# The last two stages of an eight-part transformer kernel: experts' weights merged beside layer norms, the experts' bias by a one-row matmul, sums read from PSUM, the output stored by groups

## The reference

```
x = x + L3_xattn(LN(x), ctx_2048)           # ends in LN(.) * ln_scale + ln_bias, eps 1e-6
x = x + L3_ffn(LN(x))                       # below

y1 = _ln(x + _mha(x, in_proj_w, ...), ln1_g, ln1_b)
gates = softmax(y1 @ wg)                    # 2048 x 8
idx = argmax(gates)                         # one expert for each token, 256 tokens at most for each
h = einsum('ecd,edf->ecf', disp, w1) + b1[:, None, :]
y = einsum('ecf,efd->ecd', h, w2) + b2[:, None, :]
out = where(keep, gate_val * y[slot], 0)
y2 = _ln(y1 + out, ln2_g, ln2_b)
```

## Time and profile before

| | |
|---|---|
| median of 3 runs | 4094.75 us (4091.4 to 4101.48) |
| the profiled execution | 4094.75 us, of which the span (first to last instruction) 4093.0 us |
| busy share | TensorE 89%, VectorE 66%, ScalarE 55%, GpSimd 33% |
| granted TensorE clock, mean | 0.935 of full speed |
| cross attention's end to the span's end | 3832.4 to 4093.0 us, 260.6 us or 6.4% of the span |

### The profile page before, as it was taken

The page is one execution under the profiler, slowest core; times in us unless marked ns, Lnnn a source line. Parts: engine busy times, 40 slices in busy tenths (PEclk is TensorE's granted clock), DMA queues, the critical chain, the costliest instruction groups (busy, mean ns, idle before and its releaser), DMA issues. The chain is left out here.

```text
span 4093.0 us, 72451 instructions
## 1 busy us (share of the span) xinstructions
PE 3629.6 (89%) x28012; PEld 2243.5 (55%) x28017; DVE 2716.3 (66%) x4497; ACT 2253.7 (55%) x3885; POOL 1367.2 (33%) x1655
## 2 busy tenths in 40 slices
PE   3699999889699986997889999999999999999554
PEld 2233333478444434675457776777677776776441
DVE  5799999644477736554347666666666666766648
ACT  2599999633277752222146566665666566656220
POOL 3011111230011102210035556655565556556310
PEclk7699999999799986998989999999999999999777
DMA  4422232001256401000010000000000000000010
GB/s 140 130 59 54 49 58 48 21 12 36 65 78 92 67 2 31 2 2 10 12 53 17 1 1 17 1 17 1 17 1 17 1 17 1 1 1 1 7 42 16
DMA packets 117717, 122.90 MB, mean 30 GB/s; under 512 B 19008, under 2 KB 95648, under 8 KB 116992
## 3 DMA queue, kind: packets, MB, share of 16 engines
q1 hardware_dynamic: 104184, 111.20, 12.0%
q10 hardware_dynamic: 13200, 7.16, 0.6%
HBM read 102.51 MB, written 15.68 MB: 29 GB/s over the span
## 5 line engine op out<-in xcount | busy, mean ns | idle before, releaser
L869 DVE TENSOR_REDUCE att_peak.1<-psS 128x1 f32<-128x512 f32 (+1 forms) x1024 | 579.1, 633 | 21.0 <-PE psS L744 14.7
L2098 DVE TENSOR_TENSOR att_highest.1<-att_highest.1,psS 128x1024 f32<-128x1024 f32 (+1 forms) x320 | 356.7, 1115 | 218.1 <-ACT prob_0.1 L2032 111.8
L839 ACT ACTIVATE att_probT.1<-psT 128x512 f32<-128x512 f32 (+1 forms) x682 | 366.6, 568 | 29.6 <-PE psT L773 9.6
L2190 POOL TENSOR_TENSOR key_sums_0.1<-key_sums_0.1,prob_0.1 128x512 f32<-128x512 f32 x256 | 334.5, 1306 | 28.7 <-POOL key_sums_0.1 L2190 0.4
L2190 POOL TENSOR_TENSOR key_sums_1.1<-key_sums_1.1,prob_1.1 128x512 f32<-128x512 f32 x256 | 332.3, 1298 | 32.8 <-ACT prob_1.1 L2038 5.1
L869 DVE TENSOR_REDUCE att_peak.2<-psS 128x1 f32<-128x512 f32 (+1 forms) x512 | 261.7, 568 | 79.1 <-PE psS L744 76.2
L790 PE MATMUL psM<-att_probT.1,quad_values.1 128*9 128x256 f32 (+1 forms) x3840 | 292.6, 382 | 0.2 <-issue 0.2
L744 PE MATMUL psS<-key_stack.1,query_stack.1 64*128 64x512 bf16 (+1 forms) x1024 | 253.6, 379 | 25.0 <-PEq L379 15.9
L2110 DVE TENSOR_REDUCE att_shift.4<-psO 128x4 f32<-128x512 f32 x64 | 44.3, 692 | 319.0 <-PE psO L1941 319.0
L2185 POOL TENSOR_TENSOR key_sums_0.1<-prob_0.1 128x512 f32<-128x512 f32 x64 | 81.8, 1277 | 517.2 <-ACT prob_0.1 L2038 517.2
L2119 DVE TENSOR_TENSOR prob_1.1<-prob_1.1,psO 128x1024 f32<-128x1024 f32 (+1 forms) x256 | 245.7, 1012 | 5.6 <-PE psO L1948 5.6
(11 more groups left out here) (687 smaller groups left out, 7857.2 us busy)
## 6 DMA issues: line engine op xcount, KB each, us to landing
key_stack.1<-key_parts SPq DMA_DIRECT2D x384, 58.0 KB
key_stack.2<-key_parts SPq DMA_DIRECT2D x96, 200.1 KB
ctx_rows.1<-in_ctx_dram SPq DMA_DIRECT2D x8, 1536.0 KB
key_parts<-split_parts.2 SPq DMA_DIRECT2D x8, 1200.8 KB, 7.4
ctx_keys_0.1<-in_ctx_dram ACTq DMA_DIRECT2D x4, 768.0 KB
ctx_keys_1.1<-in_ctx_dram ACTq DMA_DIRECT2D x4, 768.0 KB
query_stack.1<-query_parts SPq DMA_DIRECT2D x192, 16.0 KB
ctx_values_0.1<-in_ctx_dram SPq DMA_DIRECT2D x4, 768.0 KB
```

The lines of the kernel that those rows point to most:

```text
L839: self.k.nc.scalar.activation(probs[:, blks[0]:blks[-1] + 1, :].rearrange("p b q -> p (b q)"), bank[0:w, 0:len(blks) * S], ACT.Exp).then_i ...
L869: self.k.nc.vector.tensor_reduce(self.peak[:, 2 * h + s, c:c + 1], self.score_bank[m % 3][:, 0:w], AX_X, ALU.max).then_inc(self.peak_done. ...
L2098: self.k.nc.vector.tensor_tensor(own, old, new, ALU.max).then_inc(self.raised.sem, 1)
L2190: nc.gpsimd.tensor_tensor(acc, acc, own[:, h, c * BANK:(c + 1) * BANK], ALU.add).then_inc(self.summed.sem, 1)
```

## The change

1. `cross3` no longer loads `ln_scale` and `ln_shift` and no longer norms at its end. A new block, `two_norms_beside_experts`, takes in that norm, its scale, shift and addition to `X`, and the norm of `X` that opens `batch_attention`. The scale, shift and addition go by groups of four tiles (128x512), each followed by the `bn_stats` of its four tiles. Beside it the experts 0 to 3 are merged. SP issues all of the experts' loads (25 DMAs, 4.2 MB: 8 x 512 KB), with scale and shift as its eighth and ninth; ScalarE's queue issues the eleven loads that SP issued before, ahead of the square root.
2. The attention itself is as it was.
3. `norm_beside_experts` does the norm with `ln1_g`, `ln1_b` by groups of four tiles and the transposes of a group as soon as it is ready, with experts 4 to 7 merged beside it.
4. The block that loads `wgate` and `b2` and the merging block are gone. Merging now alternates buffers: the next expert's w1 is transposed before the product of this one, ScalarE copies both products, GpSimd spreads b1, and b2 goes in by a matmul of one row of ones with the row of b2.
5. `apply_experts`: each half of a tile is a 128-row matmul and a second one of one row (ones, 1 x 128, with the merged bias row, 1 x 512) into the same bank; VectorE's eight scaled sums read PSUM, without a copy to SBUF, and the tile's `bn_stats` for the last norm follows them.
6. `last_norm` has no statistics of its own, goes by groups of four tiles, and stores each group (256 KB) when it is added.

The core of the diff:

```
 def cross3 ...
-                     (scale[:], rows(d["L3_xattn_ln_scale"])), (shift[:], rows(d["L3_xattn_ln_bias"]))]
...
-        layer_norm(k, 1e-6, src=k.XN, transposed=False)
-        scale_and_shift(k, k.XN, scale, shift, add_to=k.X)
...
+def dve_scale_and_shift(k, link, norm, g, scale, shift):
+    for t in range(4 * g, 4 * g + 4):
+        last = norm.dve_apply(t)
+    link(last)
+    x = four_tiles(k.XN, g)
+    link(k.nc.vector.tensor_tensor(x, x, over_four(scale), ALU.mult))
+    return k.nc.vector.tensor_tensor(x, x, over_four(shift), ALU.add)
...
+class MergedExperts:
...
+    def pe_product(self, pe, e):
+        nc, out = self.k.nc, self.k.psT[:, e % 2, :]
+        pe.wait_ge(*self.w1_copied(e + 1))
+        if e >= 2:
+            pe.wait_ge(*self.w12_copied(e - 1))
+        for f in range(FT):
+            nc.tensor.matmul(out[:, 0:D], self.w1T[:, e % 2, f, :], self.w2[:, e, f, :], start=(f == 0), stop=(f == FT - 1))
+        pe.wait_ge(*self.b1_spread(e + 1))
+        for f in range(FT):
+            nc.tensor.matmul(out[:, D:2 * D], self.b1x[:, e % 2, f, :], self.w2[:, e, f, :], start=(f == 0), stop=False)
...
+        nc.tensor.matmul(out[:, D:2 * D], self.ones[:], self.b2[:, e * D:(e + 1) * D], start=False, stop=True).then_inc(self.w12_done.sem, 1)
...
+def two_norms_beside_experts(k, experts, scale, shift, loads):
...
+        @block.sync
+        def _(sp):
+            for e in range(2):
+                experts.load(sp, e)
+            for dst, src in ((scale, "L3_xattn_ln_scale"), (shift, "L3_xattn_ln_bias")):
+                sp.dma_start(dst[:], rows(k.dram[src])).then_inc(affine_loaded.sem, 16)
+            for e in range(2, E):
+                experts.load(sp, e)
...
+            old.dve_variance(dve, link)
+            old.dve_invert(dve, link)
+            dve.wait_ge(*affine_loaded(32))
+            for g in range(NT // 4):
+                link(dve_scale_and_shift(k, link, old, g, scale, shift))
+                x = four_tiles(k.X, g)
+                link(nc.vector.tensor_tensor(x, x, four_tiles(k.XN, g), ALU.add))
+                for t in range(4 * g, 4 * g + 4):
+                    last = new.dve_stats(t)
...
+        @block.scalar
+        def _(act):
+            for dst, src in loads:
+                act.dma_start(dst, src).then_inc(loaded.sem, 16)
+            old.act_deviation(act)
+            experts.act_turned(act, 0)
+            experts.act_run(act, 0, EARLY)
...
+        @block.tensor
+        def _(pe):
+            experts.pe_run(pe, 0, EARLY)
+            for g in range(NT // 4):
+                pe.wait_ge(*xn_done(g + 1))
+                turn_tiles(k, pe, g, xt_done)
...
 def apply_experts ...
-                        pe.wait_ge(*biased(n - 3))
-                    nc.tensor.matmul(k.psS[:, n % 4, :], k.XT[:, t * P:(t + 1) * P], w12[:, i * BANK:(i + 1) * BANK],
-                                     start=True, stop=True).then_inc(product.sem, 1)
+                        pe.wait_ge(*added(EB * (n - 3)))
+                    own = slice(EB * i, EB * i + EB)
+                    out = k.psS[:, n % 4, :].rearrange("p (e d) -> p e d", d=D)
+                    nc.tensor.matmul(out, k.XT[:, t * P:(t + 1) * P], experts.both[:, own, 0, :], start=True, stop=False)
+                    nc.tensor.matmul(out, experts.ones[:], experts.both[0:1, own, 1, :], start=False, stop=True).then_inc(product.sem, 1)
...
-                    nc.vector.tensor_tensor(y[:, t % 2, i * BANK:(i + 1) * BANK], k.psS[:, n % 4, :],
-                                            b12[:, i * BANK:(i + 1) * BANK], ALU.add).then_inc(biased.sem, 1)
...
-                    nc.vector.scalar_tensor_tensor(out=x, in0=y[:, t % 2, e * D:(e + 1) * D], scalar=comb[:, t, e:e + 1], in1=x,
+                    nc.vector.scalar_tensor_tensor(out=x, in0=k.psS[:, n % 4, at:at + D], scalar=comb[:, t, e:e + 1], in1=x,
                                                    op0=ALU.mult, op1=ALU.add).then_inc(added.sem, 1)
+                dve.wait_ge(*added(t * E + E))
+                last = norm.dve_stats(t)
```

More of the change, by code:

```diff
@@ new lines, in encoder3 @@
+def encoder3(k):
+    with ExitStack() as mem:
+        affine = {n: k.sb(n, [P, D], ctx=mem) for n in ("ln1_g", "ln1_b", "ln2_g", "ln2_b")}
+        wgate = k.sb("wgate", [P, E], ctx=mem)
+        experts = MergedExperts(k, mem)
+        batch_attention(k, experts, [(t[:], rows(k.dram["L3_ffn_" + n])) for n, t in affine.items()] + [(wgate[:], k.dram["L3_ffn_wg"])])
+        norm_beside_experts(k, experts, affine["ln1_g"], affine["ln1_b"])
+        gates, comb = k.sb("gates", [P, NT, E], ctx=mem), k.sb("comb", [P, NT, E], ctx=mem)
+        softmax_gates(k, mem, wgate[:], None, gates)
+        place_in_order(k, mem, gates, comb)
+        norm = Norm(k, mem, 1e-5, k.XN)
+        apply_experts(k, mem, comb, experts, norm)
+        last_norm(k, norm, affine["ln2_g"], affine["ln2_b"])
@@ L2255, in scale_and_shift, with last_norm @@
+def last_norm(k, norm, scale, shift):
+    nc, chain, ready, stored = k.nc, k.flag("dve_chain"), k.flag("x_added"), k.flag("stored")
+    GROUPS = NT // 4
     with nc.Block() as block:
@@ L2258, in _ @@
             link = Chain(dve, chain)
[L2260 to L2265, removed]
-            link.end()
[L2269 to L2278, removed]
+            norm.dve_variance(dve, link)
@@ L2280, in _ @@
+            norm.dve_invert(dve, link)
+            for g in range(GROUPS):
+                link(dve_scale_and_shift(k, link, norm, g, scale, shift))
+                x = four_tiles(k.X, g)
+                nc.vector.tensor_tensor(x, x, four_tiles(k.XN, g), ALU.add).then_inc(ready.sem, 1)
+            link.end()
         @block.scalar
         def _(act):
-            for g in range(NT // 4):
-                act.wait_ge(*xt_done(g + 1))
-                nc.scalar.copy(k.XT[:, g * BANK:(g + 1) * BANK], k.psS[:, g, :]).then_inc(xt_copied.sem, 1)
@@ L2304, in batch_attention, with _ @@
-def batch_attention(k, loads):
+            norm.act_deviation(act)
+        @block.sync
+        def _(sp):
+            out = k.out.rearrange("b (t p) d -> p (b t) d", p=P)
+            for g in range(GROUPS):
+                sp.wait_ge(*ready(g + 1))
+                sp.dma_start(four_tiles(out, g), four_tiles(k.X, g)).then_inc(stored.sem, 16)
+            sp.wait_ge(*stored(16 * GROUPS))
+def batch_attention(k, experts, loads):
     nc = k.nc
@@ L3538 @@
 STAGES = (cross0, ffn0_and_cross1, coupled1, depool2, latent2, cross3, encoder3,)
-def store(k):
-    nc, stored = k.nc, k.flag("stored")
-    with nc.Block() as block:
-        @block.sync
-        def _(sp):
-            sp.dma_start(k.out.rearrange("b (t p) d -> p (b t) d", p=P), k.X[:]).then_inc(stored.sem, 16)
-            sp.wait_ge(*stored(16))
 def layers_kernel(nc, dram, out, place):
@@ L3570, in layers_kernel @@
             stage(k)
-        store(k)
 _OUT = ((B, S, D), "float32")
```

286 lines of the change are left out of this document (190 added, 96 removed).

## The result

| | before | with the change |
|---|---|---|
| median | 4094.22 us (6 runs, 4091.4 to 4101.48) | 4111.66 us (6 runs, 4102.62 to 4115.19) |
| ratio, 95% interval | | 1.0037 [1.0027, 1.0048] |
| profiled execution | 4094.75 us, span 4093.0 | 4108.38 us, span 4106.4 |
| mean granted clock | 0.935 | 0.926 |

The change is slower, by 0.37%. The forecast was 4090 us with a range of 4072 to 4110; the measured median lies 1.7 us above it.

The account below looks back on a forecast made before the run. VectorE was taken to bound the apply stage (busy 64.44 of 70.7 us). Terms −0.7 + 2.6 + 1.0 − 1.9 − 4.1 − 38.0 + 40.9 − 4.7 = −4.9 from 4094.75 gave 4089.9, say 4090; range 4072 to 4110.

Parts of the forecast that it names:

- the price of the one-row matmul in the apply stage: Apply stage: one-row records cost the same as full ones, 0.855 us at half clock; stage 111.2 us, +40.9.
- Rival 2: Apply stage: changing stationary operand between 128 rows and one costs 0.58 us per half, 18.6 us; total 4108.5; chance 0.10.
- The clock: Apply stage: pairs of one full and one one-row matmul, begun at clock 0.50, stay at 0.50.
- rival 1: Apply stage: clock rises to full after the first tile, stage 59.9 us, total 4039; chance 0.16.
- The rows in use matter: TensorE: busy time alone neither holds nor brings the high clock, shown by 32-row and 64-row matmuls near 0.50.
- The output norm's wait: Block of the two norms: first apply waits for a later root and for scale and shift, +2.6 (+1.6 to +8).
- The queue stall of the earlier trace: Cross attention's start: SP's fourth issue, 4.51 us, stalls whatever it loads; the start's term was −0.7.
- The merging: Merging block ahead of the apply stage: removed, less a barrier, its work covered by the two norm blocks, −38.0.
- the load block: Block between the last copy and the first gate matmul: 4.44 us less one barrier, −4.1.
- the encoder's norm: Encoder's norm by groups: VectorE +1.0, only the last group's transposes and copy behind it −2.9, together −1.9.
- the end: From the last sum to the span's end: 18.5 us instead of 23.25, −4.7 (−6 to −3).
- Rival 3: Norm blocks: merging delays transposes and SP's queue stalls before scale and shift; 4099.5 us, inside the forecast's range, no own chance.

Follow-up runs that it names:

- e5: The change with eight unread 128-row matmuls of 512 columns ahead of the apply stage's first pair, as a warm start: 4115.66 us, ratio 1.0051.
- e10: The change with both matmuls of each half on 64 rows, leaving the upper 64 features out of the experts' products: 4092.62 us, ratio 0.9991.
- e3: The change with TensorE's order altered: for each tile two full matmuls, then the two one-row ones: 4050.62 us, ratio 0.9884.
- e9: The change with a 128-row bias matmul, scale and shift first on SP's queue, five ScalarE loads moved to SP's end: 4036.74 us, ratio 0.9859.

## Why the prediction was wrong

**The step that failed** is the price of the one-row matmul in the apply stage: "I price the one-row matmul like the full one", 32 × 4 × 0.855. The rows it rested on, have few-row records one behind the other, with no full-row matmul between them. The records themselves are no dearer (1136 ns against 1141), but each change between 128 rows and few costs 0.29 us at half clock, because the next weights are not loaded beside the running matmul. Two changes for each of 32 halves are 18.9 us: +59.8 instead of +40.9. The sum without this term was −45.8, measured −44.6, so nearly the whole miss is this one term.

**Rival 2 had it**, mechanism and size: 0.58 us for a half from the earlier trace rows, 0.59 measured; 4108.5 us for the total, 4108.38 in the profiled run and 4111.66 at the median. I gave it 0.10. What I held against it, that those 8-row matmuls might be waiting for something else, is not borne out. The rows showed 0.95 and 1.05 us where 0.855 was due, and no wait stands beside them. TensorE's weight loads at the same place, in the trace of the kernel before, have the pattern of the changed kernel: two loads at once, at the start of their own matmul, after a pause of the loader.

```profile
1955.67 0.29 PEld L1712 LDWEIGHTS psT<-combT.1,tables.1 8*128 8x128 f32 x2 [0.76 <-issue]
```

A price seen in three rows of the same trace deserved the main sum. That it fits so closely is partly luck, though. At full clock two changes cost 0.40 us here (e5), not the 0.29 of the earlier trace rows, and half clock makes that 0.59, some 1.5 times as much and not twice. The low start and the doubling cancel.

**The clock** was called rightly: 0.50 in the whole stage, and rival 1 did not come. But the reason given carries only half of it. Its rows, show streams of few-row matmuls alone, and for those it stands after e10. For pairs with a full matmul in each the step from these rows was a guess, and that it came true was in part luck: e3 has the same matmuls in another order and the full clock. The rows of rival 2 spoke against it, too. There two full matmuls and one of 8 rows follow each other in turn, and the window over them, in the trace of the kernel before, has the full clock:

```profile
1953.00:1966.00 13.00, 12.23 (x25) 4.17 (x26) 4.24 (x7) 3.35 (x5) 0.00 (x0) 1.00 0.00 0
```

"The rows in use matter" was also too smooth a picture: 64 rows in use bring no more than one, and 65 as much as 128. The Trainium skill's rule (TensorE: Matmul & The Clock Gate, Part 1), that the clock goes by how busy the array has been, does not hold here if busy means occupied in time: TensorE was busy in 128 of 130 us, at 0.50. Counting only full-row work as busy would fit e10, but does not by itself tell the change from e3, which has just as much of it. Whether the order or the gaps make that difference stays open.

**The hidden costs.** The output norm's wait was +5.1 in place of +2.6, within its bounds (+1.6 to +8): the root alone made 2.6 of it, where 1.6 was expected, the shift landed 7 us after its issue, and e9 takes the 5 us back by reordering the queues. I had put ScalarE's 0.64 MB and SP's 1.05 MB through at the pace of one store, and the shift came later than that pace gives. The queue stall of the earlier trace rows is not bound to what is loaded: in the changed kernel the fourth issue of the same block took 4.22 us with other data. But a fourth place does not stall everywhere: in the new block of the two norms SP's fourth issue took 0.29 us. What brings the stall stays open. The merging, the load block, the encoder's norm and the end came within 1 us of their terms. (The upper bounds add up to 4105, not 4104, and the eight 32-row items of the earlier trace rows are records, so four matmuls; neither changes the forecast.) Rival 3 did not happen; no transpose that mattered waited for an expert.

**The chances.** 0.07 for slower was too low by the price in the earlier trace rows: taken into the sum it gives 4108.5.

## What to carry to other kernels

Before adding a small matmul between full ones, count the changes of the stationary operand between more than 64 rows and fewer, and find a row of the trace where that happens: here each cost 0.3 us at half and 0.2 us at full clock. Padding such a matmul to more than 64 rows costs nothing in records, takes the changes away and lets the clock rise; here that turned a ratio of 1.0037 into 0.9865. If it can't be padded, group the small ones, so that the changes are few: two and two gave 0.9884.

## What the runs showed of the hardware

- Between 64 and 65 rows of a stationary operand of 128 columns, with fp32 matmuls of 512 columns: 2.00 us a matmul and a clock of 0.50 with 64 rows, 0.86 us and full clock with 65.
- The same matmuls in another order get another clock: pairs one by one, 0.50 for 130 us (and a full clock that they were given is lost within 9 us); two and two, 1.00 from the third tile on; and in the kernel before, two full ones to one of 8 rows, 1.00. Why, and whether the order or the gaps at the changes decide, was not tried and stays open.
- The moving operand read in runs of 128 columns at a stride of 256 took the same time as one run of 512 (stage 130.1 us in both, at half clock).
- A change between 128 rows and few costs 0.29 us at half clock (the change, e3) and 0.20 us at full clock (e3, e5), and the weights of the next matmul are loaded only as the one before ends.
